# Rolling the ten trips of a round into an inner loop of register-counted pairs

## The reference

```python
xn = layernorm(x)
x = x + relu(segment_sum((xn @ W_gnn)[src] * w, dst)) + linear_attention(xn)
h = layernorm(x)
for _ in range(30):
    h = h + 0.01 * tanh(h)
    h = h * sigmoid(h)
    h = layernorm(h, ln_w, ln_b) @ W.T + b
out = x + h
```

## Time and profile before

| what | value |
|---|---|
| median of 3 runs | 4656.01 us (4652.26 to 4659.70) |
| the profiled execution | 4659.7 us |
| its span, first to last instruction | 4657.9 us |
| mean granted TensorE clock | 0.976 of full speed |
| stage F | from about 860 us to the end |
| PE busy over the span | 89% |
| DVE, ACT, POOL busy | 80%, 76%, 69% |

### The profile page before, as it was taken

How to read it: one execution, slowest core, us unless ns; L and a number is a source line. 1 busy time by engine, 2 the same in 40 slices (tenths; PEclk the granted TensorE clock), 3 DMA queues, 4 the chain that set the end, 5 groups by cost and what they waited for, 6 DMA issues and landing times.

```text
span 4657.9 us, 92135 instructions
## 1 busy us (share of the span) xinstructions
PE 4166.0 (89%) x28680; PEld 3768.5 (81%) x28680; DVE 3737.4 (80%) x7288; ACT 3527.8 (76%) x5199; POOL 3229.6 (69%) x3713
## 2 busy tenths in 40 slices
PE   0377776899999999999999999999999999888888
PEld 0254444799999989999989999999999999888888
DVE  4355555688888888888888888889888888888888
ACT  3222111688888888888888888888888889888887
POOL 1455455588888888888888888888888886444444
PEclk9699998899999999999999999999999999999999
DMA  6433333222222232222232222223222221100000
GB/s 201 136 108 110 103 103 94 73 78 78 77 73 77 77 97 74 77 78 77 73 97 77 77 73 77 77 77 95 76 78 77 72 78 54 45 1 1 1 1 23
DMA packets 229860, 352.03 MB, mean 76 GB/s; under 512 B 78161, under 2 KB 168382, under 8 KB 229406
## 3 DMA queue, kind: packets, MB, share of 16 engines
q0 software_dynamic: 82496, 224.47, 16.6%
q1 hardware_dynamic: 142873, 117.94, 8.8%
q10 hardware_dynamic: 4037, 3.95, 0.3%
HBM read 307.30 MB, written 38.91 MB: 74 GB/s over the span
## 4 chain that ended last, share of the span: by engine, by line
PE 64%; DVE 17%; issue 6%; another core or an unknown queue 5%; ACT 4%; DMA 2%; POOL 2%; DVEq 0%; SPq 0%; ACTq 0%; POOLq 0%
PE MM L1368 37%; PE TR L1360 11%; PE AGG L1255 11%; DVE st L1110 4%; DVE T L1142 4%; PE XB L1267 3%; DVE v_low L1155 3%; ACT T L750 3%; DVE hot L994 1%; POOL gat L532 1%; DVE k_ss L1011 1%; PE MM L1291 1%; DMA a_x<-in_x 1%; PE XB L1261 1%
## 5 line engine op out<-in xcount | busy, mean ns | idle before, releaser
L532 POOL DMA_INDIRECT gat<-xn_d,src_cur x1700 | 1693.4, 996 | 689.2 <-issue 450.0
L1368 PE MATMUL MM<-w_high,v_high 128*125 128x256 f32 x5040 | 1465.8, 291 | 0.0
L1368 PE MATMUL MM<-w_low,v_high 128*125 128x256 f32 x5040 | 1417.8, 281 | 0.0
L1368 PE MATMUL MM<-w_high,v_low 128*125 128x256 f32 x5040 | 1416.9, 281 | 0.0
L1142 DVE SCALAR_TENSOR_TENSOR T<-T,MM 125x1024 f32<-125x1024 f32 x725 | 884.7, 1220 | 409.0 <-ACT T L750 404.7
L765 ACT ACTIVATE T<-T,sh,rs 125x256 f32<-125x256 f32 x2102 | 1109.5, 593 | 23.8 <-DVE sh L1120 20.2
L1110 DVE BATCH_NORM_STATS2 st<-T 125x6 f32<-125x512 f32 x1500 | 989.4, 701 | 6.1 <-issue 5.1
L1255 PE MATMUL AGG<-gat,hot 128*125 128x256 f32 x3400 | 865.6, 386 | 125.9 <-issue 67.0
L1368 PEld LDWEIGHTS MM<-w_high,v_high 128*125 128x125 f32 x5040 | 940.2, 187 | 0.0
L497 POOL TENSOR_TENSOR rs<-ve,minus_half 125x4 f32<-125x4 f32 x755 | 787.0, 1042 | 218.8 <-DVE ve L1115 207.0
L1368 PEld LDWEIGHTS MM<-w_low,v_high 128*125 128x125 f32 x5040 | 937.7, 186 | 0.0
(11 more groups left out here) (176 smaller groups left out, 2953.3 us busy)
## 6 DMA issues: line engine op xcount, KB each, us to landing
gat<-xn_d,src_cur POOLq DMA_INDIRECT x1700
k_x<-xn_d SPq DMA_DIRECT2D x100, 125.0 KB
g_u<-gen_d SPq DMA_DIRECT2D x100, 125.0 KB
g_x<-in_x SPq DMA_DIRECT2D x100, 125.0 KB
a_x<-in_x SPq DMA_DIRECT2D x24, 512.0 KB, 5.4
xn_d<-a_n SPq DMA_DIRECT2D x24, 512.0 KB, 3.9
x_cur<-x_d SPq DMA_DIRECT2D x25, 448.0 KB
out_rows<-x_cur SPq DMA_DIRECT2D x25, 448.0 KB
```

The costliest lines, as they stand in the source:

```text
L532: pool.indirect_dma_start(gat[c][:], None, xn_d, bass.IndirectOffsetOnAxis(ap=src_cur[e][:, c:c + 1], axis=0)).then_inc(S(f"gathered{c}"), 16)
L1368: last = mm(MM[b][0:R, t // 2, t % 2 * D:(t % 2 + 1) * D], rows_, w, start=k == 0, stop=k == len(products) - 1)
```

## The change

The ten trips of a round become an inner hardware loop of four iterations with two trips each, over a register `u`, and behind it two more trips that stand alone. This holds for all five engines and for all five rounds. In rounds 0 to 2 the inner loop lies in the loop over `r`, so that a trip's number is made from two registers; in rounds 3 and 4 it is made from `u` and a constant. The order of the work, the buffers, the waits and their values are the same. The work that belongs to a round's end (`end`, `last`) stands only in the second of the two trips behind the loop.

```diff
             with eng.Fori(0, LAST_G) as r:
-                for u in range(TRIPS):
-                    body(r * TRIPS + u, u % 2, r, u, u == TRIPS - 1, True, True, False)
+                with eng.Fori(0, TRIPS // 2 - 1) as u:
+                    for h in range(2):
+                        body(r * TRIPS + u * 2 + h, h, r, u * 2 + h, False, True, True, False)
+                for h in range(2):
+                    body(r * TRIPS + (TRIPS - 2 + h), h, r, TRIPS - 2 + h, h == 1, True, True, False)
             for r in range(LAST_G, ROUNDS):
                 more = r < ROUNDS - 1
-                for u in range(TRIPS):
-                    end = u == TRIPS - 1
-                    body(r * TRIPS + u, u % 2, r, u, end, more and not end, more, not more and end)
+                with eng.Fori(0, TRIPS // 2 - 1) as u:
+                    for h in range(2):
+                        body(u * 2 + (r * TRIPS + h), h, r, u * 2 + h, False, more, more, False)
+                for h in range(2):
+                    body(r * TRIPS + TRIPS - 2 + h, h, r, TRIPS - 2 + h, h == 1, more and h == 0, more, not more and h == 1)
```

## The result

The changed kernel takes 4691.23 us by the median of 7 runs (4666.44 to 4700.16); the kernel before, run beside it, 4656.01 us (4643.62 to 4662.72). The ratio is 1.0072, with a 95% interval of 1.0049 to 1.0093: slower by 35 us. The forecast was 4731 us, with a range of 4693 to 4775. The direction was right, and 75 us were forecast for 35.

The account below looks back on a forecast made before the run. TensorE was taken to bound rounds 0 to 3, with little slack on any engine in round 4. Misses of 60 and 12 us plus 3 for register steps made 75 us, so 4731 us, range 4693 to 4775.

Parts of the forecast that it names:

- The bound and the mechanism: TensorE bounds rounds 0 to 3, round 4 has little slack anywhere; 15 taken inner-loop branches each fetch code and stall TensorE.
- The choice between 0.2 and 5.2 us: Cost of TensorE's taken inner branch: 0.2 us if its 9.5-block body is kept, 5.2 if not; 5.2 was taken.
- the price of one miss in rounds 0 to 3: Each of 12 inner branches in rounds 0 to 3 costs 5.0 us, between 2.6 and 6.9; together 60 us.
- The forecast's pieces: At the two present branches: idle 3.13 and 3.17 us, transposes 1.05 more, matmuls 0.60 and 1.87 more; 4.8 and 6.1 together.
- lower bound of 2.6 per branch: Least price of a miss in rounds 0 to 3: idle time less half a microsecond, with no fall of the clock.
- Round 4: Three inner branches cost 4 us each, between 1.9 and 5.4, 12 us together; 1.9 idle and 1.65 to 2.9 for clock.
- Register steps: Steps computing trip numbers lie bare only behind a miss: 0.2 us at each of 15 branches, 3 us (bounds 0 and 0.8).
- The other engines: Misses of ScalarE, GpSimd and VectorE at the branches stand parallel to TensorE's stall and are already in the 5.0 us.
- the "some": Unspecified addition in the upper bound: 12 x 6.9 + 3 x 5.4 + some = 105 to 120 us, so 4775.
- the body was not kept: Rival: TensorE keeps the inner body, each branch costs 0.21 us, 3 us in all; 4659 us, no change; chance 0.07.
- nothing got faster: Rival: body kept and code stops streaming through F, 40 looped trips give back 6 to 12 us; 4647 us; chance 0.02.
- no sequencer was bound: Rival: register steps bind TensorE's sequencer, 5 us bare in 24 trips of rounds 0 to 2 add 120; 4851 us; chance 0.05.

Follow-up runs that it names:

- the loop over 20 slots: Kernel before, but TensorE alone runs the first eight trips of round 4 as a loop over 20 slots; stage F 3782.7 us in one execution.

## Why the prediction went wrong

*The bound and the mechanism* were right. TensorE sets the pace of stage F, the 15 new branches are taken, and each fetches code. The choice between 0.2 and 5.2 us, made by proportion from bodies of 1.6 and 47.5 blocks, came out on the right side, and by luck as far as the proportion goes (5.9 against 5); now it has rows: 5.3 blocks are kept, 8.0 and 9.5 are not. What the prediction quoted from the Trainium skill, 128 KiB for TensorE (Runtime: NRT & Kernel Launch, "Instruction fetch mechanics"), fits: 5.3 blocks are 87 KB, and 8.0 are the whole 128 KiB, which would leave no room for a block fetched ahead. The same section of the Trainium skill also says that a taken branch has to fetch when its target is outside the current window of two blocks. The traces here do not agree with that: the loop over 20 slots branched back five times over 5.3 blocks, and q8 moved none. I go by the measurement.

*The step that failed is the price of one miss in rounds 0 to 3*: 5.0 us, measured 2.5, so 60 us were forecast and 30.0 came. It was taken from the two branches at rounds' ends and carried to the middle of rounds. Two things differ there, and both were in the trace. At a round's end the output is stored; the earlier trace rows show 294 and 220 GB/s behind the branches, a mean of 80 over a round. With the stores made small the same two branches take 3.8 us. And since the work queued ahead lasts the same 2.6 us from the start of every branch, one that is 1.1 us shorter leaves a third less idle time (4.13 and 2.12 us at 3573, against 5.21 and 3.13), after which the clock mostly stays up: it fell behind 3 of 15 and not behind each. Over all the profiles here it fell behind 11 of the 12 branches that left 3 us or more idle, and behind 16 of the other 64. The forecast's pieces were 3.15 for idle time, 1.7 to 2.9 for the clock; over the twelve they measured 2.0 and 0.3 in the mean, and 0.2 for transposes that are slower even where the clock stays up. So of the 2.5 us that are missing the idle time accounts for 1.1 and the clock for most of the rest. Its lower bound of 2.6 per branch, "the idle time less half a microsecond, with no fall of the clock", kept the idle time of a round's end and was therefore above the mean.

*Round 4*: 4 us a branch, measured 2.3 (6.9 in all against 12), and less with the shorter trips between, for the same reason: the branches take 3.3 to 3.7 us. The forecast left 1.9 us bare beyond the wait for the low part. At the branch of 4306 us it is 0.5:

```profile
4308.53 1.20 DVE v_low L1160
4309.73 0.48 issue
4310.22 1.04 PE TR L1365 x8
```

And the clock fell behind one of three.

*Register steps* were to cost 3 us behind the misses. From a branch's end to the next transposes it is 0.48 us in the kernel before and 0.48 to 0.63 behind the inner branches, so they cost at most 0.15 each. Between the branches looped trips of rounds 0 to 3 are as short as before (the odd ones last 77.5 us in both), so there they are free. The price of a kept branch in round 4, some 0.2 us with the steps behind it, is what was assumed.

*The other engines*: the prediction said that their misses lie beside TensorE's and make no odds. Beside TensorE's miss that is so: 36.9 us with them, 41.7 without. But it took them for free, and they aren't: alone they cost 18 us. That matters for whoever repairs TensorE's part only.

*The range* ended at 4693, by a lower bound that was no bound; the median of 4691.23 lies under it. At the other end the terms add up to 99 us, and the "some" that makes 105 to 120 of them has no row. *The rivals*: the body was not kept, nothing got faster, and no sequencer was bound.

## What to carry to other kernels

Before a loop is rolled, ask for each engine how long its body is against what has been seen to stay; a body that is kept costs 0.2 us a turn, one that isn't 3.3 to 5.6 us less the work that is queued. Price a stall in the surroundings where it will occur: the same branch was a third longer beside the output's stores, and since a longer idle time costs the clock as well, the price grows faster than the stall. Stalls of several engines at one place are paid once, and taking the longest away uncovers the next.

## What was not expected

GpSimd also stalled for 2.43 us behind the inner branch of round 1 that falls through (at 2278 us with ScalarE, GpSimd and SyncE rolled), and not behind those of rounds 0 and 2.

The part before stage F, the same code in all kernels here, lasted from 861.9 to 899.1 us. That spread is as large as the change's whole effect, and only the profile's own windows took it out.
